# A slot kernel on one core: Gram form of the channel attention, an opening in a written order, gate and up ahead of the routing weights

## What is computed

```python
x = x + attn_a(layernorm(x));  x = x + ffn(layernorm(x))
x = x + attn_b(layernorm(x));  x = x + ffn(layernorm(x))

# attn_a, per batch, 8 heads of 16 channels
xn = x * rsqrt(mean(x*x) + eps) * norm_weight
q, k, v = split(xn @ w_qkv.T)                 # each 512 x 128
q, k = l2norm over the 512 tokens of each channel; q *= exp(temperature)
attn = softmax(q_h.T k_h)                     # 16 x 16 per head: channels, not tokens
out = (attn v_h).T @ w_out.T

# ffn: 8 experts of 336 hidden units, the first k of 8 by probability
probs = softmax(x @ router_w.T); k = argmax(actor(x)) + 1      # actor: gelu, tanh form
out = sum_e scores_e * ((silu(x @ gate_e.T) * (x @ up_e.T)) @ down_e.T)

# attn_b: 512 x 512 scores, a piecewise factor on them, softmax, v, projection
```

## Time and profile before

| | |
|---|---|
| median of three runs | 533.92 us (532.71 to 534.98) |
| the profiled execution | 536.83 us |
| its span, first to last instruction | 535.0 us |
| TensorE busy | 507.4 us, 95% |
| VectorE, GpSimd, ScalarE busy | 351.5, 278.8, 243.8 us |
| mean granted clock of TensorE | 0.971 of full |
| HBM traffic | 7 MB, nearly all in the first 20 us |

### The profile page before, as it was taken

The page is one execution under the profiler, slowest core; times in us unless marked ns, Lnnn a source line. Parts: engine busy times, 40 slices in busy tenths (PEclk is TensorE's granted clock), DMA queues, the critical chain, the costliest instruction groups (busy, mean ns, idle before and its releaser), DMA issues.

```text
span 535.0 us, 6598 instructions
## 1 busy us (share of the span) xinstructions
PE 507.4 (95%) x2125; PEld 358.1 (67%) x2125; DVE 351.5 (66%) x773; ACT 243.8 (46%) x406; POOL 278.8 (52%) x268
## 2 busy tenths in 40 slices
PE   3779899999999999999989999999998999999996
PEld 2456667666767776777756777667775777666663
DVE  3454846466289989579994699966989454653332
ACT  3443372534563657425756147652383523522221
POOL 4122655565465465653655355482464645665553
PEclk9785899999999999999999999989999999999999
DMA  8400000000000000000000000000000000000000
GB/s 284 159 2 0 1 1 1 1 0 1 0 2 0 1 1 1 1 1 1 1 1 0 1 0 2 1 0 1 21 1 0 1 16 5 0 2 20 0 1 20
DMA packets 7774, 7.38 MB, mean 14 GB/s; under 512 B 700, under 2 KB 7612, under 8 KB 7740
## 3 DMA queue, kind: packets, MB, share of 16 engines
q1 hardware_dynamic: 7740, 6.97, 4.1%
HBM read 5.91 MB, written 1.05 MB: 13 GB/s over the span
## 4 chain that ended last, share of the span: by engine, by line
PE 83%; DVE 10%; issue 3%; ACT 1%; POOL 1%; DMA 1%; DVEq 0%; POOLq 0%
PE bank L1011 24%; PE bank L885 15%; PE bank L887 15%; PE bank L886 15%; PE bank L1062 3%; PE bank L902 2%; PE bank L979 1%; PE bank L912 1%; DVE t L819 1%; PE bank L930 1%; PE bank L1050 1%; DVE xn L689 1%; PE bank L955 1%; DVE mk L844 1%; POOL rstd L458 1%
## 5 line engine op out<-in xcount | busy, mean ns | idle before, releaser
L489 POOL TENSOR_TENSOR t<-t,sl 128x512 f32<-128x512 f32 x168 | 217.3, 1299 | 195.0 <-DVE t L819 175.3
L819 DVE TENSOR_TENSOR t<-bank,sbc 128x512 f32<-128x512 f32 x168 | 114.3, 684 | 105.8 <-PE bank L887 103.3
L587 ACT ACTIVATE sl<-bank 128x512 f32<-128x512 f32 x168 | 99.8, 596 | 169.5 <-PE bank L887 140.2
L1011 PE MATMUL bank<-t,WD 128*128 128x512 f32 x336 | 172.7, 597 | 0.0
L885 PE MATMUL bank<-xhF,WGh 128*128 128x512 f32 x168 | 105.5, 628 | 0.1
L1011 PEld LDWEIGHTS bank<-t,WD 128*128 128x128 f32 x336 | 63.7, 189 | 16.8 <-issue 1.0
L885 PE MATMUL bank<-xhF,WUh 128*128 128x512 f32 x168 | 68.2, 406 | 2.2 <-DVE t L819 2.2
L887 PE MATMUL bank<-xhF,WUl 128*128 128x512 f32 x168 | 67.4, 401 | 0.0
L886 PE MATMUL bank<-xlF,WUh 128*128 128x512 f32 x168 | 67.3, 401 | 0.0
L887 PE MATMUL bank<-xhF,WGl 128*128 128x512 f32 x168 | 66.9, 398 | 0.0
L886 PE MATMUL bank<-xlF,WGh 128*128 128x512 f32 x168 | 66.7, 397 | 0.0
(11 more groups left out here) (170 smaller groups left out, 679.9 us busy)
## 6 DMA issues: line engine op xcount, KB each, us to landing
stage<-in_gate SPq DMA_DIRECT2D x7, 192.0 KB, 5.1
stage<-in_up SPq DMA_DIRECT2D x7, 192.0 KB, 5.4
WD<-in_down SPq DMA_DIRECT2D x7, 192.0 KB, 5.4
X<-in_x SPq DMA_DIRECT2D x4, 256.0 KB, 4.5
out<-X SPq DMA_DIRECT2D x4, 256.0 KB, 2.3
raw<-in_small SPq DMA_DIRECT2D x1, 580.0 KB
rows<-in_row SPq DMA_DIRECT2D x1, 136.0 KB, 4.3
cols<-in_columns SPq DMA_DIRECT2D x1, 3.0 KB
```

Of the source, the lines that this page charges most:

```text
L489: pool.tensor_tensor(t2[k % NT2][:, :], t2[k % NT2][:, :], sl[k % NSL][:, :], ALU.mult).then_inc(a_done, 1)
L587: act.activation(sl[k % NSL][:, :], bank[k % 2][:, :], ACT.Silu).then_inc(silu_done, 1)
L819: dve.tensor_tensor(t2[k % NT2][:, :], bank[2 + k % 2][:, :], sbc[k // CH % 2][:, :], ALU.mult).then_inc(t2_done, 1)
L1011: pe.matmul(OACC[:, :], WD[:, c, :], t2[k % NT2][:, :], start=(c == 0), stop=(c == CH - 1))\
```

## The change

It has three parts.

1. **Gram form.** For channel attention only `xn.T xn` of a batch is needed (`ag`, 128 x 128), then `ar` = Gram times the q and k weights (256 columns), `asim` = similarity from `ar`, and the sums of squares as two one-column products of `qsq` = `ar` times the weights, elementwise (VectorE). On the way out attention, output weight and v weight are multiplied into one matrix `mixw` (`awo`, `am`, `am2`), which `y` applies to the transposed input. `aqk`, `av`, `aT`, `aav` and their evictions go; the transposed v weight `wv` is made once.
2. **Opening in a written order.** `PRELUDE` lists the steps before slot 0: attention of batch 0, normalization of block F0 and Gram and transpose of batch 1, two weight pieces, with the weight splits for the rest (`swh`, `swl`) behind attention's first steps. Slots begin when `xl` of F0 is done. The rest of batch 1 (`A1_STEPS`), the routing of F0 (`F0_STEPS`) and pieces 2 to 20, one at the end of each slot, lie inside the slots. The first load of small weights is split in two; all transfers are issued at once in a fixed order.
3. **Gate and up ahead of the routing.** VectorE's product is now up bank times `sl` (step `uk`, it waits for silu), GpSimd's is times `sbc` (step `um`). `um` and `down` have their own pace: `products` takes up to two of each per slot, `um` when `sbc` of the block is there and a running count of GpSimd's time allows it, `down` 1.6 slots behind. `t2` has sixteen buffers in place of six. silu's buffer is freed by VectorE and not by GpSimd.

```diff
-LAG = 3
-NSL, NT2 = 2, 6
+AFTER_POOL = 1.6
+NSL, NT2 = 2, 16
...
-A_STEPS = [(0, "stats"), (1, "xn"), (3, "xT"), (5, "aqk", 0), (6, "aqk", 1), (8, "av"), (10, "asim"),
-           (10, "ass"), (12, "ascale"), (14, "asT"), (14, "amax"), (15, "aexp"), (17, "aT"),
-           (19, "aav"), (21, "y")]
+PRELUDE = [("stats", "A", 0), ("xn", "A", 0), ("ag", 0), ("xT", "A", 0), ("ar", 0), ("wph", 0), ("wph", 1),
+           ("asim", 0), ("ass", 0), ("wpl", 0), ("swh", 0), ("wv", 0), ("ascale", 0), ("asT", 0),
+           ("amax", 0), ("aexp", 0), ("awo", 0), ("am", 0), ("stats", "A", 1), ("wpl", 1), ("am2", 0),
+           ("y", 0), ("stats", "F", 0), ("xn", "A", 1), ("ag", 1), ("xn", "F", 0), ("xT", "F", 0),
+           ("xT", "A", 1), ("xl", "F", 0), ("swl", 0)]
+A_STEPS = [(0, "stats"), (1, "xn"), (3, "ag"), (4, "xT"), (5, "ar"), (8, "asim"), (9, "ass"), (10, "ascale"),
+           (12, "asT"), (13, "amax"), (14, "aexp"), (15, "awo"), (17, "am"), (19, "am2"), (21, "y")]
+A1_STEPS = [(1, "ar"), (3, "asim"), (4, "ass"), (5, "ascale"), (6, "asT"), (7, "amax"), (7, "aexp"), (8, "awo"),
+            (9, "am"), (11, "am2"), (13, "y")]
+F0_STEPS = [(0, "route"), (1, "rexp"), (1, "inner", 0), (2, "inner", 1), (2, "rsum"), (3, "rrank"), (4, "tanh"),
+            (5, "gelu"), (7, "act"), (7, "actk"), (10, "sbc")]
...
-A_STARTS = (-42, -26, 1, 21)
+A_STARTS = (9, 25)
 B_STARTS = (25, 48, 67, 90)
 M_START = 7
-PIECES_FROM, PIECES_LEFT = 5, 12
-
-GU_AFTER = {("tanh", 0): 0, ("act", 0): 1}
...
-    threads = [thread("F", n, F_STEPS, CH * n - F_AHEAD) for n in range(2 * NB)]
+    threads = [thread("F", n, F_STEPS, CH * n - F_AHEAD) if n else thread("F", 0, F0_STEPS, 0) for n in range(2 * NB)]
...
-    threads += [thread("A", b, A_STEPS, A_STARTS[b]) for b in range(NB)]
-    pieces = [("wp", j) for j in range(NPIECES)]
+    threads += [thread("A", 1, A1_STEPS, 0)] + [thread("A", b, A_STEPS, A_STARTS[b - 2]) for b in range(2, NB)]
+    pieces = [("wp", j) for j in range(2, NPIECES)]
...
+        if s[0] in POOL_COST:
+            pool_free[0] = max(pool_free[0], k) + POOL_COST[s[0]] / 2.25
...
-    k = A_STARTS[0] - 1
+    def products(k, most):
+
+        for _ in range(most):
+            j = len(um_end)
+            if ("uk", j) in done and ("sbc", j // CH) in done and pool_free[0] < k + 1:
+                add(("um", j))
+                um_end.append(pool_free[0])
+            if downs[0] < len(um_end) and um_end[downs[0]] + AFTER_POOL <= k:
+                add(("down", downs[0]))
+                downs[0] += 1
+
+    k = -1
+    for s in PRELUDE:
+        assert ready(s), s
+        add(s)
     while k < last - 1:
-        if k + 1 < 0 or (k + 1) % CH or ("sbc", (k + 1) // CH) in done:
+        if (k + 1) % CH or ("xl", "F", (k + 1) // CH) in done:
             k += 1
+            add(("gu", k))
+            assert k < NT2 or ("down", k - NT2) in done
+            add(("uk", k))
         else:
             for th in threads:
                 th[0] -= th[0] <= k
-        if k >= 0 and ("um", k) not in done:
-            if k >= 2:
-                add(("gu", k))
-            add(("um", k))
-            if k >= LAG:
-                add(("down", k - LAG))
+        products(k, 2)
...
                 pe, act, dve = pe + cost[0], act + cost[1], dve + cost[2]
-        if pieces and (k >= 0 or k >= A_STARTS[0] + PIECES_FROM and len(pieces) > PIECES_LEFT):
+        if pieces:
             add(pieces.pop(0))
         debt = [max(0.0, act - pe), max(0.0, dve - pe)]
     assert not any(th[1] for th in threads)
-    for k in range(last, last + LAG):
-        add(("down", k - LAG))
+    while downs[0] < last:
+        k += 1
+        products(k, 2)
...
-            sp.dma_start(raw[:, :], small_d).then_inc(small_loaded, 16)
-            sp.dma_start(cols[:, :], cols_d).then_inc(small_loaded, 16)
+            sp.dma_start(raw[:, 0:C_OUT], small_d[:, 0:C_OUT]).then_inc(qkv_loaded, 16)
+            sp.dma_start(cols[:, :], cols_d).then_inc(qkv_loaded, 16)
+            for j in range(2):
+                sp.dma_start(stage[j][:, :], (gate_d, up_d)[j][:, 0:WCOLS]).then_inc(stage_loaded[j], 16)
+            sp.dma_start(raw[:, C_OUT:C_ALL], small_d[:, C_OUT:C_ALL]).then_inc(small_loaded, 16)
             sp.dma_start(X[:, NT:2 * NT, :], xv[:, 1]).then_inc(x_loaded[1], 16)
             sp.dma_start(rows[:, :], rows_d.partition_broadcast(P)).then_inc(rows_loaded, 16)
-            sp.dma_start(w2[:, 0:KMAX], w2_d).then_inc(small_loaded, 16)
...
                 if kind == "um":
                     k = s[1]
+                    if k % CH == 0:
+                        wait_free(pool, turn_of["sbc", k // CH])
                     pool.wait_ge(t2_done, k + 1)
-                    pool.wait_ge(silu_done, k + 1)
-                    pool.tensor_tensor(t2[k % NT2][:, :], t2[k % NT2][:, :], sl[k % NSL][:, :], ALU.mult).then_inc(a_done, 1)
+                    pool.tensor_tensor(t2[k % NT2][:, :], t2[k % NT2][:, :], sbc[k // CH % 2][:, :], ALU.mult).then_inc(a_done, 1)
...
+                if kind == "swh":
+                    act.wait_ge(small_loaded, 16)
+                    act.activation(SWh[:, 0:2 * P], raw[:, C_BQKV:C_BQKV + 2 * P], ACT.Copy)
+                    act.activation(SWh[:, 3 * P:4 * P], raw[:, C_ACTOR:C_ALL], ACT.Copy)
+                    act.activation(router[:, 0:E], raw[:, C_ROUTER:C_ROUTER + E], ACT.Copy).then_inc(swh_ready, 1)
+                    act.activation(bq[:, :], cols[:, 1:2], ACT.Copy, scale=B_SCALE).then_inc(bq_ready, 1)
...
                     t = turn_of[s]
                     wait_full(act, t)
                     if n >= 2:
-                        act.wait_ge(t2_done, CH * (n - 1))
+                        act.wait_ge(a_done, CH * (n - 1))
                     act.activation(sbc[n % 2][:, :], m_bank(t)[:, :], ACT.Copy).then_inc(n_free(t), 1)
                 if kind == "gu":
                     k = s[1]
                     act.wait_ge(g_full, k + 1)
                     if k >= NSL:
-                        act.wait_ge(a_done, k - NSL + 1)
+                        act.wait_ge(t2_done, k - NSL + 1)
...
+                    dve.wait_ge(gw_ready, b + 1)
+                    dve.tensor_tensor(qsq[:, :, :].rearrange("p r c -> p (r c)"), m_bank(t)[:, 0:2 * P],
+                                      raw[:, C_QKV:C_QKV + 2 * P], ALU.mult).then_inc(n_free(t), 1)
...
+                        wait_full(dve, turn_of["am", b - 1])
+                    else:
+                        dve.wait_ge(small_loaded, 16)
                     dve.reciprocal(ari[:, :], ars[:, :]).then_inc(ari_ready, 1)
+                    dve.wait_ge(ari_ready, b + 1)
+                    dve.tensor_scalar(wo[:, :], raw[:, C_OUT:C_OUT + P], ari[:, 0:1], None, ALU.mult).then_inc(wo_ready, 1)
...
-                if kind == "um":
+                if kind == "uk":
                     k = s[1]
-                    if k % CH == 0:
-                        wait_free(dve, turn_of["sbc", k // CH])
                     dve.wait_ge(u_full, k + 1)
+                    dve.wait_ge(silu_done, k + 1)
                     if k >= NT2:
                         dve.wait_ge(down_done, k - NT2 + 1)
-                    dve.tensor_tensor(t2[k % NT2][:, :], bank[2 + k % 2][:, :], sbc[k // CH % 2][:, :],
+                    dve.tensor_tensor(t2[k % NT2][:, :], bank[2 + k % 2][:, :], sl[k % NSL][:, :],
                                       ALU.mult).then_inc(t2_done, 1)
...
+                if kind == "ag":
+                    b = s[1]
+                    t = turn_of[s]
+                    pe.wait_ge(xn_ready, norm_no["A", b] + 1)
+                    xn = xns[norm_no["A", b] % 2]
+                    m = turn(t)
+                    for i in range(NT):
+                        r = pe.matmul(m[:, 0:P], xn[:, i, :], xn[:, i, :], start=(i == 0), stop=(i == NT - 1))
+                    r.then_inc(m_full[t % 3], 1)
+                if kind == "ar":
+                    b = s[1]
                     t = turn_of[s]
                     if b == 0:
                         pe.wait_ge(wn_ready, 1)
+                    wait_free(pe, turn_of["ag", b])
+                    pe.matmul(turn(t)[:, 0:2 * P], gram[:, :], raw[:, C_QKV:C_QKV + 2 * P], start=True, stop=True)\
+                      .then_inc(m_full[t % 3], 1)
+                if kind == "asim":
+                    b = s[1]
+                    t = turn_of[s]
+                    m = turn(t)
+                    wait_free(pe, turn_of["ar", b])
+                    pe.matmul(m[:, 0:P], raw[:, C_QKV + P:C_QKV + 2 * P], gw[:, 0, :], start=True, stop=True)
+                    for j in range(2):
+                        r = pe.matmul(m[:, P + j:P + j + 1], qsq[:, 1 - j, :], ones[:, :], start=True, stop=True)
+                    r.then_inc(m_full[t % 3], 1)
+                if kind == "asT":
+                    b = s[1]
...
+                if kind == "am":
+                    b = s[1]
+                    t = turn_of[s]
```

(16 more changed lines are left out.)

189 lines of the change are left out of this document (84 added, 105 removed).

## The result

The changed kernel takes 568.75 us in the median (566.03 to 570.94), the kernel before 534.45 beside it: ratio 1.064, interval 1.058 to 1.070. It is slower by 34.3 us. The forecast was 533.0 with a range of 518 to 544, so the time lies outside it and on the other side of the likeliest case.

The account below looks back on a forecast made before the run. TensorE was taken to bound the kernel. Gate 15 at 80.4, plus 452.2 remaining, 2.5 for slots without `down` and -1 steady gave a 534.1 us span, 535.9 profiled, 533.0 by the median's ratio; range 518 to 544.

Parts of the forecast that it names:

- What bounds the kernel: Whole kernel: TensorE, busy 95% of the span; work taken from it at 60 to 525 us is time.
- the Gram form: Channel attention: TensorE's work falls from 7.3 to 3.5 us a batch; batches 2 and 3 give 7.6 us.
- the start of the slots: Opening: the shorter chain of batch 0 brings the first gate product to 28.8 us, for 38.66.
- What the slots lose: First 15 slots: every third gate waits for VectorE's low half; gates 3, 6, 9 at 41.9, 50.9, 61.5 us.
- gate 12: Slot 12: `xn` of batch 2 (1.1 us) and the low half on VectorE put this gate product at 72.0 us.
- The remaining 452.2: Behind gate 15 (80.4 us): TensorE's 480.4 us less 28.2 already done; later `down`s cost nothing in themselves.
- The hole without `down`: Near slot 27 GpSimd runs dry; some seven slots have no `down`: 2.5 us lost, between 0 and 6.
- The steady term: Steady part: silu no longer waits for GpSimd, `uk` stops VectorE at table loads; -1 us, bounds -5 to +8.
- the forecast's 23.4 of stops: First 15 slots: TensorE does 28.2 us of work in 51.6; the stops take 23.4 us.
- the 25.8 by which 509.2 lay under the old span: Whole kernel, TensorE never stopped: first gate 28.8, then 479.7 plus 8.3 moved in, less 7.6; 509.2 us against 535.0.
- The second: Rival, chance 0.28: beyond the opening VectorE becomes the bound, `uk` waiting for silu behind exp blocks; 537 to 547 us.
- wrong high if TensorE's waits past the twentieth slot exceed 8 us: Sign set beforehand, past slot 20: TensorE's waits above 8 us there would show the prediction wrong high.

Follow-up runs that it names:

- g_only: Kernel before with the Gram form of channel attention alone; order, roles, pieces and buffers as they were: 526.97 us, ratio 0.986.
- a_even_xn: Changed kernel, two pieces in slots 0 to 2, GpSimd paced by gate/up products, one `down` a slot at distance 14, GpSimd's products behind `xn`: 540.36 us.
- a_paced_xn: a_paced with GpSimd's products standing behind `xn` and waiting for it in slots that normalize: 540.07 us, ratio 1.011.
- a_paced: a_ahead with GpSimd's products of a slot waiting for that slot's gate product (the second for its up product): 544.40 us, ratio 1.018.
- g_roles: g_only with silu's product on VectorE, the routing weights' on GpSimd and sixteen buffers; routing still first, distance 3: 530.73 us, ratio 0.993.
- a_ahead: Changed kernel with two weight pieces a slot instead of one in slots 0 to 2: 548.43 us, ratio 1.027.
- a_px_early: a_paced_xn with attention of batches 2 and 3 begun at slots 5 and 21 in place of 9 and 25: 539.93 us, ratio 1.013.
- g_only_xn: g_only with GpSimd's products behind `xn` and waiting for it in slots that normalize: 526.36 us, ratio 0.988.
- g_roles_xn: g_roles with GpSimd's products behind `xn` and waiting for it in slots that normalize: 530.09 us, ratio 0.993.

## Why the prediction was wrong, point by point

**What bounds the kernel, the Gram form, the start of the slots** were right. The first gate product was to come at 28.8 and came at 29.96. The Gram form was put at 7.6 us and gave 7.2, but the agreement is closer than it deserves: the 7.6 are for batches 2 and 3 beside full work, and g_only holds the shorter attention of batches 0 and 1 too, so the term alone isn't measured.

**What the slots lose** was right up to gate 9, in its cause and nearly in its numbers: TensorE's waits for the low half were 3.36, 1.51 and 3.76 against 3.5, 2 to 4 and 4.2. The chain ahead of gate 3, in the timeline of ScalarE and VectorE of the changed kernel (against the earlier trace rows):

```profile
39.74 1.28 ACT L615 ACT_TABLE_LOAD   x1
41.03 0.60 ACT L615 ACTIVATE sl<-bank 128x512 f32<-128x512 f32 x1
...
41.73 0.69 DVE L858 TENSOR_TENSOR t<-bank,sl 128x512 f32<-128x512 f32 x1 [1.42 <-ACT sl L615]
42.34 0.41 DVE L751 TENSOR_TENSOR qsq<-bank,raw 128x256 f32<-128x256 f32 x1
42.67 0.55 DVE L742 TENSOR_TENSOR WUl<-stage,WUh 128x384 fp32r<-128x384 f32 x1
```

It is the chain of the forecast, silu, `uk`, `qsq`, low half. Silu ends 1.7 us and gate 3 starts 1.4 us later than forecast, 1.2 of them brought along from the first gate product. The silu starts 1.29 us behind the start of its table load. The Trainium skill (ScalarE: Activation LUTs, What ACT_TABLE_LOAD costs) has a drain of some 1380 ns on top. It doesn't show here either, and the 4.1 us that it would have added up to gate 9 did not come.

The first step that failed is **gate 12**. I gave `xn` of batch 2 its 1.1 us and the low half 0.55, from rows of before, where GpSimd had at most one product to run. From slot 12 the changed kernel has a backlog of twelve. I knew it: the forecast has GpSimd start its products there, "two a slot (1.29 each against slots of 3.1)". That was the planner's pace taken for the queue's. The two steps took 6.5 us instead of 1.65, gate 12 came at 76.2 for 72.0, and gate 15 at 87.4 for 80.4.

**The remaining 452.2** is the second step that failed, and where most was lost. It was forecast as 452.2 + 2.5 - 1 = 453.7 us and took 479.8: 26.1 more. Together with the 7.0 at gate 15 these are the 33.1 by which the span of 567.2 lies above 534.1. TensorE is busy for 452.4 of them (at a clock of 0.98, for 0.99 before), as long as I had put for work and known stops together, and it stands for the other 27.4. The waits of TensorE by line of the changed kernel show that no single one carries it; the first row lies for 16.3 us ahead of gate 15:

```profile
PE bank L924 <- DVE WUl L742: 20.5, 6, 7.7
...
PE bank L941 <- DVE xn L717: 4.9, 4, 2.6
PE bank L1025 <- DVE hq L831: 4.3, 3, 1.7
PE bank L924 <- DVE t L858: 4.1, 4, 1.9
PE bank L924 <- DVE xlS L737: 2.9, 1, 2.9
```

Past the pieces the releasers are mostly VectorE's steps, one after another. The sentence "all cover in this stretch was made of `down`s before; they now come later, which costs nothing in itself" is right by a_even_xn against a_paced_xn only for where they stand. What I didn't see is that the distance gives GpSimd work to run at any time, and that VectorE's steps beside it cost three to four times their price (`xn` 1.2 to 1.3 us for 0.34): holding GpSimd back gave 4.0 and 4.3 us (a_paced, a_paced_xn). That is what the runs show to be its doing; some of it lies ahead of gate 15, and how the rest of the 26.1 divides isn't shown.

**The two smaller terms.** The hole without `down` was put at 2.5: closing it brought nothing (a_even_xn 540.36, a_paced_xn 540.07). The steady term was put at -1 between -5 and +8, "nearer to the gain"; g_roles against g_only gives +3.8, inside the bounds and on the other side. In the changed kernel VectorE waits for silu, but about as long as GpSimd did before:

```profile
DVE t L858 <- ACT sl L615: 19.8, 10, 2.8
```

I take the difference to be that behind VectorE's wait there are steps for which TensorE waits, and behind GpSimd's only `down` three slots on. That is argued; no run tests it.

**The sum by the runs.** From 534.2 to 568.75, by medians: Gram form -7.2 (g_only); roles +3.8 (g_roles); the lead with its opening +17.7 (a_ahead); one piece a slot instead of two at first +20.3. The last is about the forecast's 23.4 of stops. Against these I had set a gain from the lead of 18.2 (the 25.8 by which 509.2 lay under the old span, less the Gram form's 7.6). That gain is what is missing: with its opening the lead doesn't give 18.2, it takes 17.7. Of these, holding GpSimd to the slots gives back 4.0 and keeping `xn` free of it 4.3. 9.4 us stay (540.07 against 530.73).

The windows above split these 9.4 by their profiled executions (539.9 against 530.4, 9.5): in the first 60 us TensorE stands 2.4 less, behind them 7.8 more, and it is busy 4.1 longer at a mean clock of 0.962 against 0.976. So a start that is 12 us earlier (gate 0 at 29.4 for 41.1, gate 3 at 37.4 for 54.0) turns into 2.4 us of TensorE's time: the gate products of the lead stand where attention of batch 1 and the routing stood before, and those come later in their turn.

What makes the 7.8 isn't settled. The hole isn't it, nor late attention of batches 2 and 3 (a_px_early). Where it arises can be read from windows cut at gates 42 and 84, by which both kernels have made the same 81 `down`s. First g_roles, then a_paced_xn; the third pair is VectorE's time for the steps on the mask between the two gates:

```profile
160.70:291.10 130.40, 124.76 (x541) 88.57 (x540) 107.95 (x217) 69.86 (x112) 72.29 (x61) 0.99 0.00 1
291.10:530.40 239.30, 231.58 (x964) 161.65 (x962) 149.28 (x288) 98.17 (x157) 126.46 (x104) 0.99 0.02 5
```
```profile
146.90:295.00 148.10, 138.30 (x565) 94.49 (x563) 123.04 (x234) 70.36 (x115) 89.31 (x73) 0.97 0.00 1
295.00:539.90 244.90, 235.24 (x975) 164.84 (x973) 150.79 (x289) 100.69 (x162) 124.76 (x103) 0.98 0.02 5
```
```profile
160.70:291.10 130.40, 38.90 (x64) 0.99 0.00 1
146.90:295.00 148.10, 52.54 (x63) 0.97 0.00 1
```

Up to gate 42 a_paced_xn has stood about as long as g_roles (25.1 us for 25.7) and comes 13.8 us earlier only because it has worked less. Between the gates it pays that back and stands 9.8 us for 5.6. VectorE is busy 15 us longer there, nearly all of it on the mask, where GpSimd's products now lie. So one candidate is the collision again, moved from `xn` to the mask; no run kept the mask free. The other is the second block: its routing hangs on `y` of batch 1, which comes at slot 14 in place of 1, so that its `sbc` comes at slot 32 for 18, and all of its steps, attention's and the backlog of `down`s lie over each other up to about slot 80. That was not tried by itself either. Both are argued, not shown, and neither explains the 5.6 us that are lost behind gate 84. In a_px_early, which takes as long, nothing is lost there (239.3 us, as g_roles) and more between the gates. Nor is it shown whether the 4.1 us in which TensorE is busy longer, at the lower clock, come of the stops.

**The rivals.** The second, VectorE as the bound beyond the opening, named the direction and the engine, and its sign was right at 0.28. But its mechanism, silu behind the exp blocks, is worth at most the 3.8 us of the roles, and its 537 to 547 misses the time by 22 us, so that it had the direction by luck in part. Nothing in the forecast had VectorE's steps get longer. The case "wrong high if TensorE's waits past the twentieth slot exceed 8 us" is what happened: from gate 21 on TensorE stands 24 us. The range was too narrow by one omission: the costs of stops and of slots were taken as known at the prices of before, in an order that puts other engines beside them.

## What to carry to other kernels

A planner's pace holds for an engine only if its queue waits for something at that pace: a distance given to a product on GpSimd turns into a burst, and beside the burst VectorE's normalizations took 1.2 us a step instead of 0.34. Price such steps at one product each, and after freeing one kind look where the products have gone. A lead must be paid in TensorE's own idle time to be worth anything: count what it stands less, not how much earlier the first product comes (here 12 us earlier, 2.4 less standing). When one part of a change is free of order and the others aren't, run it alone first: the Gram form gives 526.97 us here, 1.4% under the kernel before, and all that was built around it takes that and more.

## What the runs showed of the hardware

A VectorE `tensor_scalar` of 128x128 from SBUF to SBUF takes 0.34 us in the median with GpSimd quiet (a_paced_xn) and 1.2 to 1.3 us beside GpSimd products of 128x512, which themselves stay at 1.3. A mask step of 128x512 in bf16 takes 0.42 us by itself and up to 1.5 beside such products (a_paced_xn, 184.84 us). With the old order a third of the `xn` time is already such waiting: 28.4 us in g_only, 18.4 in g_only_xn. A GpSimd power of 128x2, 0.7 to 1.1 us long, blocks nothing that can be measured (VectorE busy 350.7 for 351.5 us). And an engine's freed time need not be worth anything: 7 us less on VectorE in g_only_xn (346.4 for 353.9) and in g_roles_xn (351.3 for 358.2) gave 0.6 us each.
